# Weighing the values of two key chunks in one burst of matmuls, every second step, in the cross attention of a two layer decoder

## The reference

```
q = x @ w_q + b_q;  k = context @ w_k + b_k;  v = context @ w_v + b_v
scores  = einsum('bqhd,bkhd->bhqk', q, k) / sqrt(8)
weights = softmax(scores, axis=-1)
out     = einsum('bhqk,bkhd->bqhd', weights, v).reshape(B, 256, 128) @ w_o + b_o
```

## Time and profile before

| what | us |
|---|---|
| median of three runs | 4210.55 (4205.43 to 4215.28) |
| the profiled execution | 4211.14 |
| its span, first to last instruction | 4209.1 |
| one step of the loop of the first cross attention | about 93.8 (1243.94 to 1337.70) |
| granted clock of TensorE, mean over the span | 0.944 |

### The profile page before, as it was taken

The page is one execution under the profiler, slowest core; times in us unless marked ns, Lnnn a source line. Parts: engine busy times, 40 slices in busy tenths (PEclk is TensorE's granted clock), DMA queues, the critical chain, the costliest instruction groups (busy, mean ns, idle before and its releaser), DMA issues. The chain is left out here.

```text
span 4209.1 us, 109822 instructions
## 1 busy us (share of the span) xinstructions
PE 3603.7 (86%) x39651; PEld 1800.8 (43%) x39651; DVE 2896.4 (69%) x3938; ACT 2384.8 (57%) x4687; POOL 1032.1 (25%) x1818
## 2 busy tenths in 40 slices
PE   4777599999999999997699583999999999999987
PEld 2444244343343434443466482443444334344435
DVE  4555677777777777784544696777777777777753
ACT  2444266666666666675233440666666666666663
POOL 3333232122222321221366102122212212221200
PEclk7889699999999999998799796999999999999998
DMA  2222222222222223221000002222222222222200
GB/s 73 57 54 53 58 56 55 68 60 53 60 51 51 56 53 73 59 50 27 1 0 0 1 0 49 59 51 56 56 69 60 52 60 50 52 55 67 55 21 20
DMA packets 222502, 200.19 MB, mean 48 GB/s; under 512 B 86918, under 2 KB 184444, under 8 KB 221964
## 3 DMA queue, kind: packets, MB, share of 16 engines
q1 hardware_dynamic: 221964, 193.04, 19.7%
HBM read 25.59 MB, written 2.10 MB: 7 GB/s over the span
## 5 line engine op out<-in xcount | busy, mean ns | idle before, releaser
L627 ACT ACTIVATE cross_Pr<-cross_sT 128x512 f32<-128x512 f32 (+1 forms) x3584 | 1833.4, 563 | 886.1 <-PE cross_sT L542 884.5
L691 DVE TENSOR_REDUCE cross_nm<-cross_ring 128x2 f32<-128x802 f32 x2048 | 1974.6, 991 | 492.5 <-PE cross_ring L508 482.7
L542 PE MATMUL cross_sT<-cross_Q,cross_K 64*128 64x256 bf16 x13312 | 1050.8, 274 | 111.3 <-ACT cross_Pr L627 40.7
L561 PE MATMUL cross_oT<-cross_Pr,cross_V 128*9 128x256 f32 x13312 | 1038.7, 383 | 0.6 <-issue 0.6
L542 PEld LDWEIGHTS cross_sT<-cross_Q,cross_K 64*128 64x128 bf16 x13312 | 514.1, 95 | 869.3 <-ACT cross_Pr L627 694.7
L508 PE MATMUL cross_ring<-cross_K,cross_Q 64*128 64x401 bf16 x4096 | 666.4, 338 | 38.3 <-DVE cross_nm L691 17.2
L436 POOL TENSOR_TENSOR cross_mp<-cross_nm,cross_one 128x8 bf16<-128x8 f32 x128 | 26.0, 203 | 1471.0 <-DVE cross_nm L696 1470.8
L561 PEld LDWEIGHTS cross_oT<-cross_Pr,cross_V 128*9 128x9 f32 x13312 | 198.4, 88 | 427.7 <-issue 247.3
L508 PEld LDWEIGHTS cross_ring<-cross_K,cross_Q 64*128 64x128 bf16 x4096 | 200.5, 94 | 170.6 <-DVE cross_nm L691 113.7
L700 DVE TENSOR_REDUCE self_nm<-self_ring 128x4 f32<-128x1024 f32 x128 | 156.7, 1224 | 141.2 <-PE self_ring L515 141.1
L1243 DVE TENSOR_TENSOR moe_rc<-moe_r,moe_bank 128x512 f32<-128x512 f32 x128 | 87.9, 687 | 169.3 <-ACT moe_r L1134 169.3
(11 more groups left out here) (326 smaller groups left out, 3370.8 us busy)
## 6 DMA issues: line engine op xcount, KB each, us to landing
cross_K<-cross_kparts SPq DMA_DIRECT2D x1152, 100.1 KB, 2.3
cross_C<-in_ctx_dram SPq DMA_DIRECT2D x32, 576.0 KB
cross_Q<-cross_qparts SPq DMA_DIRECT2D x288, 64.0 KB, 2.1
self_Q<-self_qparts SPq DMA_DIRECT2D x144, 64.0 KB, 2.1
self_K<-self_kparts SPq DMA_DIRECT2D x144, 64.0 KB, 2.1
cross_xs<-X SPq DMA_DIRECT2D x32, 128.0 KB, 2.1
X<-in_x_dram SPq DMA_DIRECT2D x4, 512.0 KB, 6.1
self_xs<-X SPq DMA_DIRECT2D x16, 128.0 KB, 2.1
```

What stands on the lines that cost most here:

```text
L542: mm = pe.matmul(sT[0:r, cfg.sT_bank(rb, u + j), (c % 2) * S:(c % 2 + 1) * S], K[ROWS * j:ROWS * (j + 1), pair, t, s:s + r], Q[ROWS * j:RO ...
L561: mm = pe.matmul(oT[32 * j:32 * j + VR, 0:S], V[0:r, rb % VB, c, 4 * g + j, :], Pr[0:r, slot, (c % 2) * S:(c % 2 + 1) * S], start=(c == 0) ...
L627: act.activation(Pr[0:r, u % NPR, 0:nc_ * S], sT[0:r, cfg.sT_bank(rb, u), 0:nc_ * S], ACT.Exp).then_inc(exped, 1)
L691: dve.tensor_reduce(nm4[:, g % 2, t, :, pk, blk], R.rearrange("p (j n) -> p j n", j=2)[:, :, 0:cfg.block], AX.X, ALU.max, negate=True).the ...
```

## The change

The list of bursts of the cross attention holds pairs of chunks in place of single chunks: seven bursts, the last with one chunk, in place of 13. Burst n stands in slot 3 + 2n of its quad in place of slot 3 + n. So chunks 0 and 1 are weighed in slot 3, chunks 2 and 3 in slot 5, and so on; chunk 12 stays in slot 15, which is slot 1 of the next quad. Self attention gets the same list as before, with one burst in slot 3. `Pr` has sixteen buffers in both versions. The counts that other engines wait for (`NV`, `NW`) follow from the list.

```diff
@@ -76,7 +76,7 @@
         self.max_units = 16 if self.cross else 2
-        self.bursts = [[c] for c in range(self.nch)] if self.cross else [list(range(self.nch))]
+        self.bursts = [list(range(c, min(c + 2, self.nch))) for c in range(0, self.nch, 2)]
@@ -114,7 +114,7 @@
             for n, cs in enumerate(self.bursts):
-                out.append((g * u + 3 + (n if self.cross else 0), ("PV", g, n)))
+                out.append((g * u + 3 + 2 * n, ("PV", g, n)))
             out.append((g * u + u + 1, ("EV", g)))
```

## The result

The changed kernel takes 4385.46 us (median of 4 runs, 4384.62 to 4397.38), the kernel before 4211.3 us in the same runs: ratio 1.0421, 95% interval 1.04 to 1.0443. It is 174 us slower; 185 us more were forecast, and both the time and the way it was to come about held in the main. Some small terms were off in size, and one effect had no place in the sum.

The account below looks back on a forecast made before the run. Bound: the 1.30 to 1.38 us round of B and exponential, balanced against TensorE's 1.26 us. Sum: 7.5 less 1.6, 5.9 us a step, 32 steps, 189 us; +185 after the last steps, about 4395 us, range 4335 to 4470.

Parts of the forecast that it names:

- The second chunk in slots 5 and 7 of quads 1 to 3: Six slots a step with 0.04 us of slack: +0.39 us each for the added chunk, 2.4 us a step.
- The eleven slots bound by TensorE: Odd slots already filled by TensorE's work, spread over quads 0 to 3: +0.43 us each, 4.7 us a step.
- Plain even slots give nothing back: Seventeen even slots that lose their PV stay at the 1.38 us round; TensorE idles instead, saving 0.
- Slots with projections, and slot 12 of quad 0: Slots 0 and 6 of quad 2 -0.55 us each, slot 10 of quad 0 -0.36, its slot 12 -0.1: -1.6 a step.
- Slots 12 and 13 of quads 1 to 3: Together they stay as long as the DMA chain for the row of maxima: 0 us.
- The four slots with a wait for VectorE: Slots 5, 9, 11 of quad 0 and 3 of quad 2: a later PV eats into the waits, +0.4 us a step.
- the 4 that I had taken off for the last steps: Last step of each layer, slots without A: +0.22 us instead of +0.39, some 2 us less each.
- the first: Rival: TensorE's order is the bound; 768 fewer bursts save 0.21 us each, 161 us, so 4050; chance 0.04.
- the second: Rival: hidden anyway, the next B's wait shrinks by what the odd slot grew; 4210; chance 0.02.
- the fourth: Rival: nothing absorbed, VectorE and DMA waits move with PV, 4480; or second chunk costs 0.55 us, 4487; chance 0.19.
- The third: Rival: even slots fall to the shorter 1.30 us round, 0.08 us less each, 43 us in all; 4352; chance 0.15.

Follow-up runs that it names:

- the new order: ScalarE's wait for the Pr buffer put ahead of its wait for the scores: 1.039 of the kernel before in the changed kernel, 0.9989 in the kernel before.

## Why the prediction was right, and where it was off

In the two traces I took the distance from each B to the next and summed it by place over the 32 steps, after less before.

- *The second chunk in slots 5 and 7 of quads 1 to 3*: forecast 2.4 us a step, 76 in all; 76 measured.
- *The eleven slots bound by TensorE*: forecast 151 us, 150 measured. Ten of the eleven grew by 0.43 in the median step. Slot 3 of quad 0 was not bound by TensorE to its end, as I had it: it grew by 0.27 in the median step. The two groups behind its PV start 0.61 us apart before and 0.49 after, so there was a short wait which no row marks. Its mean grew by 0.48, by the clock (below).
- *Plain even slots give nothing back*: right, -4 us over all seventeen and 32 steps, all of it in slot 0 of quad 0 behind turns of the loop. It is shown from two sides, by half exponentials (they move these slots) and by PV left out (it doesn't). The idle time ahead of B, forecast at about 350 us, came to 400.8: 315 at the end of these slots, where 321 was forecast, 40 at the end of slots 2, and 46 at the end of slots 12, which I had left out.
- *Slots with projections, and slot 12 of quad 0*: forecast -50 us, -49 measured.
- *Slots 12 and 13 of quads 1 to 3*: forecast 0, -14 measured. The DMA's wait shrank from 22.5 us to 6.9, and I had allowed nothing for it.
- *The four slots with a wait for VectorE*: forecast +12 us, +4 measured. This term was mis-sized. In slot 5 of quad 0 the row shows 0.25 us of idle time, and I let a later PV eat 0.25. Yet the slot grew by nothing in the median step. Behind PV stand two groups of two transposes. Their starts are 0.27 us apart in the changed kernel's timeline of TensorE:

```profile
1298.44 0.44 PE L577 MATMUL cross_ring<-ident_f,cross_On 128*128 128x128 f32 x2
1298.71 0.42 PE L467 MATMUL cross_ring<-ident_f,cross_xs 128*128 128x128 f32 x2
```

In the kernel before they were 0.69 apart, from the row below to 1255.43:

```profile
1254.74 0.44 PE L577 MATMUL cross_ring<-ident_f,cross_On 128*128 128x128 f32 x2
```

So the wait was 0.42: the profile has the group ahead as busy for 0.44 us, while the next one can start 0.27 after it. The 0.24 of slot 3 of quad 2 was too small in the same way: that slot is 3.39 us before and after.
- *Clock and loop*: not in the sum at all. Slots 1 and 2 of quad 0, which the change doesn't touch, grew by 15 us together, and slot 3 by 6 more than its median says. The windows below are of the changed kernel, first at the start of a step behind a turn of the loop and then of a step without one, and of the kernel before behind the same turn as the first (the columns are the window and its length, then busy TensorE, its loads, VectorE, ScalarE and GpSimd, then granted clock, DMA share and GB/s):

```profile
791.00:802.00 11.00, 9.54 (x66) 4.13 (x70) 4.36 (x5) 5.64 (x11) 0.00 (x0) 0.56 0.27 60
...
1286.90:1297.00 10.10, 8.13 (x103) 4.54 (x101) 6.39 (x9) 7.21 (x14) 0.00 (x0) 1.00 0.42 94
```

```profile
778.20:789.20 11.00, 10.22 (x98) 4.59 (x101) 5.54 (x8) 6.69 (x13) 0.00 (x0) 0.84 0.30 70
```

Where the loop turns, every second step, TensorE stands still: 2.81 us ahead of 791.11 in the changed kernel, 2.55 ahead of 778.20 in the one before. After it the granted clock is 0.56 of 2.4 GHz in the changed kernel's window, mostly the 1.2 GHz level, and 0.84 before. In the steps without a turn, but for the first of each cross attention, it was 1.00 there. It is no matter of this one pair: the two cross attentions have ten such turns, and the 11 us behind them had 0.50 to 0.69 in the changed kernel and 0.55 to 1.00 in the one before. The standstills were 2.67 to 3.45 us long and 2.55 to 2.94.

Why the clock falls lower in the changed kernel, no run took apart. Idle even slots fit the run that left PV out of them, 0.50 to 0.70, but idle time alone doesn't settle it. In the 14 us ahead of the standstills TensorE was busy 82% in the changed kernel, 98% in the one before and 86% with the pairs one slot later, and that last kernel had 0.72 to 1.00 behind them and standstills of 2.55 to 3.04 us.

So the slots were forecast at 189 us and came to 178: the waits for VectorE and the DMA made 8 and 14 less, the even slots 4 and the eleven 1 less, slots 1 and 2 of quad 0 made 15 more, and roundings 1. That the total is so near is in part luck: without the clock, which was in no term, the slots would have come to some 160. The last 4 us, to the 174 of the spans, lie outside the slots, most of them (3.5) ahead of the first step. They are not the 4 that I had taken off for the last steps. Those did not come: the last step of each layer grew by 6.2 us, though its odd slots without A took 1.52 us as forecast. Of the rivals, the first fell with the run that left 768 bursts out and gained 6 us, and the second with the result. Of the fourth the reverse came: more was absorbed than I allowed, and a second chunk cost 0.43, not 0.55. The third was a real mechanism, but not one that this change sets off: the 0.08 us is ScalarE's register instruction inside the loop, and it stayed. The rule of the Trainium skill, "TensorEngine Tiling", Key Properties, that a change of tiling mode drains TensorE agrees with the rows of this trace (0.09 and 0.12 us). Nearly half of those changes did go, and most of them from an engine that was waiting.

## What to carry to other kernels

Before work is moved between steps of a pipeline, find a step that already lacks it: if that step is as long as the others, it is bound by a round of waits, and what is moved out of it saves nothing while what is moved in is paid in full. An engine that is busy 86% of the time may be balanced against such a round to within a few hundredths of a microsecond, as here, and uneven work on it then costs the sum of all its peaks. Idle time on it is free for other work only as far as that work's own buffers go, here two halves of a ring that VectorE has to read.

## What the runs showed of the hardware that I had not expected

- Two waits ahead of one ScalarE instruction aren't alike. Exponentials start 0.64 us after B when they carry the wait for the scores themselves. They start at 0.72 when a register instruction ahead of them carries it, as in even slots of the loop, and at 0.70 when a wait instruction ahead of them does, as in the unrolled steps with the new order. So the order that is best in the loop costs 0.06 us in the unrolled steps.
- The idle time that the profile gives ahead of a TensorE group can be too small: 0.25 us shown where the distance of the starts fell by 0.42 when the wait was gone, since the modelled end of the group ahead lies behind the point where the next could start.
- After standstills of 2.55 to 3.45 us at the turns of the loop TensorE's granted clock was 0.50 to 1.00 in the mean over the next 11 us, and below 1.00 behind nineteen of the twenty turns of the two kernels. So a loop's turn can cost more than its own length: slots 1 and 2 of quad 0 took 15 us more in the kernel with the lower clock.
